# A graph layer on one core: the ring of gathered units goes from five slots to four, the ring of product buffers from three to four

## The reference, cut to what matters

```python
h = (x @ W).reshape(n, 8, 32)                 # x is layer-normalised
e = leaky_relu(a1[src] + a2[dst], 0.2)        # a1, a2: h summed against attn_l, attn_r
ex = exp(e - seg_max[dst])
alpha = ex / segment_sum(ex, dst)[dst]
out = segment_sum(h[src] * alpha[:, :, None], dst) + bias
```

## Time and profile before

| What | Value |
|---|---|
| Median of 3 runs | 2515.81 us (2507.62 to 2516.12) |
| Profiled execution, its own time | 2508.82 us |
| Its span | 2507.1 us |
| Mean granted TensorE clock | 0.889 of full speed |
| POOL busy | 1579.2 us, 63% |
| DVE busy | 1652.5 us, 66% |
| PE busy | 1946.2 us, 78% |
| Gathers (POOL, line 688) | 1612, from 77.0 to 2102.6 us |
| Steps scaled (DVE, line 1630) | 451 |
| DVE idle, waiting for POOL's announcement | 479.4 us |

### The profile page before, as it was taken

How to read it: one execution, slowest core, us unless ns; L and a number is a source line. 1 busy time by engine, 2 the same in 40 slices (tenths; PEclk the granted TensorE clock), 3 DMA queues, 4 the chain that set the end, 5 groups by cost and what they waited for, 6 DMA issues and landing times.

```text
span 2507.1 us, 32715 instructions
## 1 busy us (share of the span) xinstructions
PE 1946.2 (78%) x8711; PEld 1405.9 (56%) x8711; DVE 1652.5 (66%) x3559; ACT 962.8 (38%) x2085; POOL 1579.2 (63%) x1713
## 2 busy tenths in 40 slices
PE   8686777776776887777777678788886668899998
PEld 6454555554554555555555556666665444677776
DVE  7576766766666766676666677677777877433335
ACT  5443433333333333333333432223233546333332
POOL 5677777777777777777777777777777774000000
PEclk9889889898889788888888888898888889999999
DMA  7455555555555555555555556566555452100000
GB/s 250 137 148 149 146 146 152 146 147 148 146 144 154 145 146 151 146 144 154 145 147 151 144 161 167 158 175 167 168 166 142 135 138 75 41 19 15 16 19 27
DMA packets 164182, 330.66 MB, mean 132 GB/s; under 512 B 35700, under 2 KB 82394, under 8 KB 164014
## 3 DMA queue, kind: packets, MB, share of 16 engines
q0 software_dynamic: 78144, 220.11, 33.1%
q1 hardware_dynamic: 84418, 108.26, 14.2%
q10 hardware_dynamic: 1452, 0.38, 0.1%
HBM read 302.21 MB, written 26.39 MB: 131 GB/s over the span
## 4 chain that ended last, share of the span: by engine, by line
POOL 38%; issue 22%; PE 16%; DVE 9%; DMA 6%; POOLq 5%; DVEq 2%; ACT 1%; SPq 0%; ACTq 0%
POOL work L688 38%; PE bank L1222 7%; DMA work<-h_tab,cols 5%; POOLq L681 5%; PE bank L1212 5%; DVE work L1630 3%; PE bank L965 2%; DVE acc L1638 1%; DVE zs L1570 1%; DVEq L1551 1%; PE bank L1158 1%; DVE a2c L1572 1%; DVE a2c L1575 1%; DVE a2c L1574 0%; ACT L743 0%
## 5 line engine op out<-in xcount | busy, mean ns | idle before, releaser
L688 POOL DMA_INDIRECT work<-h_tab,cols x1612 | 1527.1, 947 | 502.0 <-issue 470.4
L1158 PE MATMUL bank<-work 128*128 128x264 f32 x3608 | 1075.6, 449 | 381.2 <-DVE work L1630 381.2
L1158 PEld LDWEIGHTS bank<-work 128*128 128x128 f32 x3608 | 773.2, 222 | 622.5 <-DVE work L1630 446.3
L1630 DVE TENSOR_TENSOR work<-work,bank 128x1024 f32<-128x1024 f32 x451 | 546.5, 1212 | 9.1 <-DVE X L1603 5.8
L791 ACT ACTIVATE bank<-a2c 128x64 f32<-128x64 f32 x226 | 51.5, 228 | 1093.7 <-DVE a2c L1577 1085.8
L1570 DVE TENSOR_REDUCE zs<-bank 128x128 f32<-128x384 f32 x226 | 125.3, 555 | 479.7 <-POOLq L677 479.4
L1464 DVE TENSOR_TENSOR work<-bank,cols 128x1024 f32<-128x1024 f32 x226 | 275.0, 1217 | 0.0
L785 ACT ACTIVATE work<-work,ones 128x1024 bf16<-128x1024 bf16 x226 | 259.5, 1148 | 7.4
L783 ACT ACTIVATE work<-work,pcol 128x1024 bf16<-128x1024 bf16 x226 | 257.4, 1139 | 10.1 <-DMA work<-dst_d 10.1
L1638 DVE TENSOR_TENSOR acc<-bank,acc 128x264 f32 x451 | 193.4, 429 | 34.9 <-PE bank L1158 32.7
L722 POOL COPY work<-acc 128x768 f32 (+2 forms) x17 | 14.0, 823 | 309.2 <-PE bank L1177 267.4
(11 more groups left out here) (300 smaller groups left out, 1929.5 us busy)
## 6 DMA issues: line engine op xcount, KB each, us to landing
work<-dst_d SPq DMA_DIRECT2D x226, 256.0 KB, 3.9
work<-h_tab,cols POOLq DMA_INDIRECT x1612
h_tab<-acc SPq DMA_DIRECT2D x49, 132.0 KB, 2.6
xnt_d<-qx_c SPq DMA_DIRECT2D x49, 128.0 KB
q2t_d<-qx_c SPq DMA_DIRECT2D x49, 128.0 KB
out<-wqkv SPq DMA_DIRECT2D x15, 384.0 KB, 2.5
X<-x SPq DMA_DIRECT2D x5, 1024.0 KB, 11.0
qx_c<-xnt_d SPq DMA_DIRECT2D x17, 128.0 KB, 3.3
```

The source lines that it names most:

```text
L688: nc.gpsimd.indirect_dma_start(out=work[:, (r * G + g) * TW:(r * G + g + 1) * TW], out_offset=None, in_=h_tab, in_offset=bass.IndirectOffs ...
L1158: ins = mm(bank[MB[n % len(MB)]][:, 0:TW], hot[b % HQ][:, s * G + g, :], M[n % MS][:, g, :], start=(g == 0), stop=(g == G - 1))
L1630: v.tensor_tensor(m, a, ex, ALU.mult).then_inc(msg_ready, 1)
```

## The change

The ring of gathered units has four slots in place of five, and the ring of product buffers four buffers in place of three. Their sum, and with it the size of `work`, is the same.

```diff
-RU = 5
-MS = 3
+RU = 4
+MS = 4
```

## The result

The changed kernel took 2519.61 us (median of 9 runs, 2515.84 to 2522.81), the kernel before in the same comparison 2513.81 us (9 runs). The ratio is 1.0022, with a 95% interval of 1.0014 to 1.0031: a fifth of a percent slower, 5.8 us. The forecast was 2517.4 us, with a range of 2506 to 2524 and no change of more than 0.5%. Both held. The term "late slots", for which the forecast had 1.6 us, came out about five times as large (7.8 us in the profile).

What follows compares the result with a forecast made beforehand. The prediction took POOL's unbroken gathers, 1.25 us each, to bound the kernel. It added 1.6 us for late slots and 0 for the rest to the median of three runs, giving 2517.4 us, range 2506 to 2524.

Steps and rivals of the forecast that it cites:

- late slots: Gathers on POOL held because a unit's slot is released too late with four slots: three units, +1.6 us.
- Bound by POOL's gathers at 1.25 us: Gather loop: POOL issues gathers without a break, 1.25 us each, and sets the loop's end; VectorE, ScalarE and TensorE follow.
- Ring of units, margin of about 4 us at first units of a batch: Slot wait before a unit's gathers: with four slots the scaling ends 4.06 us ahead in an ordinary case, median 4.9 us.
- the last gather came 10.7 us later and not within 5: Sign at the loop's end: if the forecast is right, the last gather stays within 5 us of 2102.6.
- starts further apart than 1.25 us: Sign in the gather loop: the prediction is wrong if POOL's starts are over 1.25 us apart in the middle of units.
- Announcements stay where they are: POOL's announcements that a unit is in, awaited by VectorE, don't move but for one by a tenth; wait 479 us within 5.
- Products, flag, tables: nothing: Fourth product buffer, flag read before unit 4, and shorter index row with shifted views: each adds 0 to the time.
- Rival one: Slot wait at line 682: the gather needs the sequencer's lead of about 2.5 us, +22 to +38 us; chance 0.08.
- Rival two: The 0.30 us gap before gathers is already the ring's wait; 6.25 us per unit, +499 us; chance 0.01.
- Rival three: The fourth product buffer removes unseen waits, shortening the end behind the last gather by at most 10 us; over 0.5%: chance 0.04.

Runs made afterwards that it cites:

- e2_copy_before: The kernel before run again without any edit (five unit slots, three product buffers), for a second profile; ratio 1.0002 to the kernel before.
- e4_two_products: The kernel before with two product buffers in place of three, still five unit slots; ratio 1.0000 to the kernel before.
- e6_six_slots: The kernel before with six unit slots in place of five and two product buffers in place of three; ratio 0.9981 to the kernel before.
- f1_six_slots_again: A repeat of six unit slots and two product buffers against the kernel before with five and three; ratio 0.9989.
- f2_before_again: The kernel before run once more as a second copy without any edit (five unit slots, three product buffers); ratio 0.9996 to the kernel before.
- e1_ring_only: The kernel before with four unit slots in place of five, product buffers left at three; ratio 1.0018 to the kernel before.

## Why the prediction came out as it did

**Bound by POOL's gathers at 1.25 us: right.** The end moved as the last gather moved, in the changed kernel (10.7 of 10.8 us) and with three slots (425 us of holds, 420 between the medians), and work taken from VectorE gave no more than the holds that went with it.

**Ring of units, margin of about 4 us at first units of a batch: right.** The median margin with four slots is 4.8 us in the changed kernel (4.9 forecast), and with five slots none was ever held (smallest margins 4.65, 3.79, 3.94 and 3.92 us in four profiles).

**Late slots, 1.6 us: mechanism right, size wrong, 7.8 us in the profile, 5.6 to 9.1 over four profiles with four slots.** Two inputs of that term were off. The smaller is the dispatch: the time from the release to the gather was taken at 0.5 us between bounds of 0 and 1.2, and is 0.79. The prediction says that the trace of before doesn't show it. It does, nearly: the time from the sequencer's step behind the slot wait (line 683) to the first gather is 0.754 us in the five units of before where it is shortest, and 0.753 or 0.754 in the six held ones. One of the five is unit 152, and its gather is the "0.9" at the end of its row:

```profile
L683 POOLq EVENT_SEMAPHORE  x1: 17/17/17, 841.0 to 841.0; - x1
```

```profile
841.70 0.94 POOL L688 DMA_INDIRECT work<-h_tab,cols  x1 [0.87 <-DVE work L1630]
```

The other 0.04 us lie between the end of the scaling and line 683. With 0.79 us the margins of the profile of before make 2.5 us in place of 1.6. The larger input is that one profile was read as if its margins were the kernel's. By the same rule, margins against 0.79 us, the other profiles with five or six slots give:

| Profile | sum of shortfalls at 0.79 us |
|---|---|
| before (the one read) | 2.5 |
| e2_copy_before | 5.0 |
| e4_two_products | 5.8 |
| e6_six_slots | 6.6 |
| f1_six_slots_again | 6.4 |
| f2_before_again | 2.6 |

The one that was read is the smallest of six, if only just. A count of 5 units under 1.0 us was a draw from a tail, and the text even took its sum for a ceiling ("the true sum for a given dispatch time is rather smaller").

What moves the tail in the mixing stage is where TensorE's clock is low, and that changes from one execution to the next. Unit 284 shows it, by the granted clock from 10 to 2 us before its release, in the profile of before and in that of the changed kernel (columns as above):

```profile
1491.99:1499.99 8.00, 6.68 (x37) 5.18 (x36) 7.61 (x19) 2.99 (x8) 6.17 (x7) 1.00 0.64 184
```

```profile
1498.66:1506.66 8.00, 7.25 (x28) 5.45 (x29) 6.23 (x14) 3.96 (x7) 6.14 (x7) 0.63 0.41 114
```

At 1.00 the way from first gather of unit 280 to the release was 17.6 us, at 0.63 it was 20.5; a unit is held when this way is over four units of gathering less the dispatch, some 19.2 us. The same was read for the eleven units of the mixing stage that stand four behind a tile end, in all ten profiles in which nothing but the depth of the rings was changed and there are four slots or more:

| Clock in those 8 us | cases | way over 19.2 us | way, us |
|---|---|---|---|
| 0.59 to 0.66 | 30 | 30 | 19.8 to 21.6 |
| 0.70 to 1.00 | 80 | 2 | 13.9 to 20.5 |

The total of VectorE's waits for sums doesn't tell this: it was 31.5 us in e1_ring_only, less than in any of the others with four slots, and yet its units 284, 300 and 325 stood in low stretches. Unit 391, in the finishing stage, is another case: its way was 19.9 us in all ten, at any clock, and it was held in every profile with four slots. What stays open is why the four profiles with four slots had 3 to 5 such low cases each and the six others 1 to 3, and why their holds (5.6 to 9.1 us) lie above what the six give by the rule (2.5 to 6.6): chance, or something that four slots do to the clock.

**The figure of 2517.4 us: its nearness is luck.** It started from 2515.81 us, the median of three runs of before, and nine runs beside the changed kernel gave 2513.81. The start was 2.0 us too high and the term too low, so the two errors partly cancel, and the distance of 2.2 us is smaller than what the term missed. The signs were less kind: the last gather came 10.7 us later and not within 5, and the sign "starts further apart than 1.25 us" can't judge anything, because a copy of before has 1.2534.

**Announcements stay where they are: not contradicted.** VectorE's wait for them was forecast at 479 us within 5 and came out at 460.8, outside. It was 479.5 in e1_ring_only and 464.8 and 468.0 in the two copies of before, so it swings by itself, as its wait for TensorE's sums does (32.7 us in before, 48.2 and 37.6 in its copies, 58.1 in the changed kernel), and the five were too narrow.

**Products, flag, tables: nothing, right.** Line 795 waits for nothing in the changed kernel, the first gather is at 77.1, and unit 4 began without a hold; one product buffer fewer changes nothing, and one more was run only together with four slots.

**Rival one, the sequencer's whole lead of 2.6 us: fell.** The release counts for 0.79 us in 6 units and in 199. **Rival two, the 0.30 us gap as the ring's wait: fell.** With three slots the ordinary spacing is 1.2498 us, with six 1.2504; it doesn't know the ring. **Rival three, faster by products: fell** with e4_two_products.

## What to carry to other kernels

Where a ring feeds an engine that works without a break, its depth is chosen by the smallest lead of release over reuse, not the usual one: time from first gather to release plus the restart (16 + 0.8 us here) against slots times pace (20 us) leaves 3 us, and a tile end, side work and a slow sum at once use them up. Read that tail from several executions, because one profile holds five or so events of it, and look in each for what the clock did there. The restart can be read before any unit is late, as the shortest time from the sequencer's step to its gather. And before a slot is paid for, look whether side work stands between the last input and the release: moving it behind one instruction won back 0.2 to 0.3% here (1.0022 to 1.0004, and 1.0036 to 1.0009), most of what the slot was worth.

## What the runs showed of the hardware beyond that

From the end of the instruction that a waiting POOL sequencer waits for to the start of its indirect gather are 0.79 to 0.81 us, in every held case of these traces, while in an unbroken row the gathers start every 1.25 us. That ordinary spacing averages from 1.2498 to 1.2536 us between executions, whatever the kernel; over 1611 gathers this is worth up to 6 us, as much as the change under study. The difference lies in the gathers' own recorded time and not in the gap before them: medians of 946 and 949 ns in before and its copy, with a gap of 0.305 us in both, and it holds from the beginning of the loop to its end. What sets it, these runs don't show.
